# A transformer decoder layer with a routed feed-forward: a new order for the last batches' steps on four engines

## The reference, cut to what matters

```
x = layernorm(x + linear_attention(x))            # 16 heads of 16; inner layer norm; out @ Wo
x = layernorm(x + softmax_cross_attention(x, ctx)) # 16 heads of 16
# feed-forward: 8 experts of 256 -> 512 -> 256, each token goes to its best 2
g      = gelu(xt @ wg1 + bg1);  probs = softmax(g @ wg2)
gates  = top-2 of probs
y      = sum_e gates[:, e] * (gelu(xt @ w_in[e]) @ w_out[e])
x = layernorm(x + y)
```

## Time and profile before

| what | value |
|---|---|
| median of 3 runs | 430.15 us (430.11 to 433.9) |
| the profiled execution's own time | 431.93 us |
| its span | 430.1 us (1.83 us of its time lie around the span) |
| mean granted TensorE clock | 0.923 of full speed |
| busy: PE, DVE, ACT, POOL | 81%, 72%, 52%, 51% of the span |

### The profile page before, as it was taken

How to read it: one execution, slowest core, us unless ns; L and a number is a source line. 1 busy time by engine, 2 the same in 40 slices (tenths; PEclk the granted TensorE clock), 3 DMA queues, 4 the chain that set the end, 5 groups by cost and what they waited for, 6 DMA issues and landing times. The chain is left out here.

```text
span 430.1 us, 12345 instructions
## 1 busy us (share of the span) xinstructions
PE 347.9 (81%) x4025; PEld 281.0 (65%) x4025; DVE 308.3 (72%) x912; ACT 222.1 (52%) x518; POOL 220.7 (51%) x287
## 2 busy tenths in 40 slices
PE   2977999999999999999887185759999999999200
PEld 1655777777777877777664053547899999988100
DVE  3767899888988889888777077468677666755193
ACT  3435676667666676766763045353544444444034
POOL 8335456676666766667258554643133333422273
PEclk9999999999999999999898588569999999999855
DMA  7520022220122211221012222325525322321393
GB/s 219 179 76 27 2 75 75 75 77 21 56 75 77 75 39 38 76 75 50 2 53 100 87 77 79 109 76 151 156 81 155 84 69 61 98 75 39 124 378 122
DMA packets 21387, 38.35 MB, mean 89 GB/s; under 512 B 3696, under 2 KB 11120, under 8 KB 21328
## 3 DMA queue, kind: packets, MB, share of 16 engines
q1 hardware_dynamic: 16768, 26.06, 19.8%
q0 software_dynamic: 3408, 9.41, 6.1%
q10 hardware_dynamic: 1152, 2.10, 1.3%
HBM read 24.71 MB, written 12.84 MB: 87 GB/s over the span
## 5 line engine op out<-in xcount | busy, mean ns | idle before, releaser
L575 POOL DMA_INDIRECT parts<-QKT,rows_all x39 | 37.8, 969 | 76.1 <-DVE QKT L1207 65.9
L328 PE MATMUL bank<-QS,EW 128*128 128x256 f16 (+1 forms) x384 | 62.6, 265 | 5.6 <-DVE XB L1021 5.6
L491 POOL TENSOR_TENSOR rstd<-veps,neghalf 128x1 f32<-128x1 f32 x48 | 39.6, 824 | 41.6 <-DVE veps L844 41.2
L1382 PE MATMUL bank<-EW,QV 128*128 x312 | 48.7, 273 | 1.8 <-DVE R L1199 0.8
L328 PE MATMUL bank<-XB,EW 128*128 128x256 f16 (+1 forms) x192 | 49.0, 264 | 0.0
L1199 DVE TENSOR_TENSOR R<-scratch,QV 128x512 f16<-128x512 f32 x39 | 26.7, 691 | 29.4 <-ACT scratch L764 17.9
L1126 DVE TENSOR_REDUCE NM<-bank 128x4 bf16<-128x512 f32 x64 | 39.6, 678 | 11.1 <-remote 10.1
L328 PEld LDWEIGHTS bank<-QS,EW 128*128 x384 | 37.7, 102 | 11.6 <-issue 6.1
L764 ACT ACTIVATE scratch<-bank 128x512 f32<-128x512 f32 x39 | 23.4, 600 | 40.5 <-PE bank L328 38.5
L506 POOL DMA_INDIRECT bkt<-REC,dest x32 | 32.9, 1029 | 21.3 <-issue 11.9
L699 ACT ACTIVATE rows_all<-bank 128x512 f32<-128x512 f32 x64 | 33.2, 603 | 18.2 <-remote 10.8
(11 more groups left out here) (240 smaller groups left out, 941.4 us busy)
## 6 DMA issues: line engine op xcount, KB each, us to landing
scratch<-w_in SPq DMA_DIRECT2D x8, 512.0 KB, 3.3
scratch<-w_out SPq DMA_DIRECT2D x8, 512.0 KB, 3.8
rows_all<-bkt SPq DMA_DIRECT2D x15, 262.0 KB
XC<-x SPq DMA_DIRECT2D x16, 128.0 KB, 3.3
XC<-ctx SPq DMA_DIRECT2D x16, 128.0 KB, 3.2
EW<-parts SPq DMA_DIRECT2D x8, 256.0 KB, 6.8
EW<-parts ACTq DMA_DIRECT2D x8, 256.0 KB, 7.4
out<-rows_all SPq DMA_DIRECT2D x8, 256.0 KB, 2.1
```

The source lines that it names most:

```text
L328: last = pe.matmul(dst, a(c), b(c), start=(c == 0 and i == 0), stop=(c == n - 1 and i == 2))
L491: pool.tensor_tensor(rstd[n][p][:], veps[n][p][:], neghalf[:, 0:1], ALU.pow).then_inc(s_rs[n], 1)
L575: pool.indirect_dma_start(parts, bass.IndirectOffsetOnAxis(ap=home[:, t, f:f + 1], axis=0), Y[t % 2][:, f, :], None).then_inc(s_put[t % 2] ...
L1382: last = pe.matmul(bank[4 + t % 2][:, f * D:(f + 1) * D], a[t % 2][:, h, f * P:(f + 1) * P], b[:, h, :], start=(h == 0 and i == 0 and f == 0),
```

## The change

Three lists are reordered; no computation is added or dropped. `up` is split into two calls of two hidden chunks each, so that other steps can stand between.

```diff
 # POOL, tail
-"sc:0 sc:1 pw1:15 sc:2 sc:3 sc:4 sc:5 sc:6 sc:7 sc:8 pw2:12 sc:9 sc:10 sc:11 sc:12 sc:13 sc:14 pw2:13 "
+"pw1:15 sc:0 sc:1 sc:2 sc:3 x1b:15 sc:4 sc:5 pw2:12 sc:6 sc:7 sc:8 sc:9 sc:10 sc:11 pw2:13 sc:12 sc:13 sc:14 sc:15 sc:16 "
...
 # DVE, tail
-"mx0:14 mx1:14 n1:15 mx2:14 mx3:14 R2:12 s2:12 full:0 O2T:13 nr:13 full:1 QM1:15 full:2 mx0:15 mx1:15 mx2:15 "
+"mx0:14 n1:15 mx1:14 mx2:14 mx3:14 R2:12 s2:12 O2T:13 nr:13 QM1:15 full:0 n2:12 mx0:15 mx1:15 mx2:15 "
...
-"choice1:2 low:0 choice2:2 whose:0 gate1:2 dest:2 gate2:2 low:1 whose:1")
+"choice1:2 choice2:2 gate1:2 dest:2 gate2:2 whose:0 low:1 whose:1")
...
 # PE
-            def up(t, e):
+            def up(t, e, hs=range(HC)):
...
-                for h in range(HC):
+                for h in hs:
...
-                last.then_inc(s_up, 1)
+                if HC - 1 in hs:
+                    last.then_inc(s_up, 1)
...
-                     "x2T:13 cntpre:1 gh:13 ao2:15 x2T:14 lg:1 x2T:15 gh:15 cnt:1 lg:2 turn:0 cntpre:2 up:0 turn:1 cnt:2")
+                     "x2T:13 cntpre:1 gh:13 ao2:15 x2T:14 lg:1 x2T:15 gh:15 turn:0 cnt:1 cntpre:2 lg:2 upa:0 cnt:2 turn:1 upb:0")
```

More of the change, by code:

```diff
@@ L564, in _ @@
                      "pw0:14 qn:15 n1:14 x1b:14 n2:11 nr:12 pw0:15 "
[2 rows of a table removed]
+                     "pw1:15 sc:0 sc:1 sc:2 sc:3 x1b:15 sc:4 sc:5 pw2:12 sc:6 sc:7 sc:8 sc:9 sc:10 sc:11 pw2:13 sc:12 sc:13 sc:14 sc:15 sc:16 "
+                     "pw2:14 sc:17 sc:18 sc:19 pw2:15 "
                      "sc:20 sc:21 sc:22 sc:23 sc:24 sc:25 sc:26 sc:27 sc:28 sc:29 sc:30 sc:31")
@@ L1184, in _ @@
                      "QM1:14 R1:15 s1:15 "
-                     "mx0:14 mx1:14 n1:15 mx2:14 mx3:14 R2:12 s2:12 full:0 O2T:13 nr:13 full:1 QM1:15 full:2 mx0:15 mx1:15 mx2:15 "
-                     "R2:13 n2:12 mx3:15 s2:13 ewl:15 O2T:14 nr:14 ewl:16 R2:14 n2:13 s2:14 ewl:17 O2T:15 nr:15 n2:14 R2:15 s2:15 "
-                     "choice1:1 n2:15 choice2:1 gate1:1 dest:1 gate2:1 "
-                     "choice1:2 low:0 choice2:2 whose:0 gate1:2 dest:2 gate2:2 low:1 whose:1")
+                     "mx0:14 n1:15 mx1:14 mx2:14 mx3:14 R2:12 s2:12 O2T:13 nr:13 QM1:15 full:0 n2:12 mx0:15 mx1:15 mx2:15 "
+                     "mx3:15 R2:13 s2:13 full:1 O2T:14 nr:14 full:2 n2:13 ewl:15 ewl:16 R2:14 s2:14 ewl:17 O2T:15 nr:15 R2:15 s2:15 n2:14 "
+                     "choice1:1 n2:15 choice2:1 gate1:1 dest:1 gate2:1 low:0 "
+                     "choice1:2 choice2:2 gate1:2 dest:2 gate2:2 whose:0 low:1 whose:1")
             def hidden_low(t):
@@ L1637, in emit @@
                     tile_turn(b)
-                if step == "up":
+                if step == "upa":
                     pe.wait_ge(s_tables, 1)
@@ L1641, in emit @@
                     held[b] = expert_of(b)
-                    up(b, held[b])
+                    up(b, held[b], range(0, HC // 2))
+                if step == "upb":
+                    up(b, held[b], range(HC // 2, HC))
                 if step == "cntpre":
```

## The result

| | kernel before | changed kernel |
|---|---|---|
| median of 14 runs each | 431.11 us | 438.35 us |
| ratio | | 1.0151, 95% interval 1.0118 to 1.0185 |
| profiled execution, own time | 431.93 us | 437.45 us |
| its span, mean granted clock | 430.1 us, 0.923 | 435.7 us, 0.921 |

What follows compares the result with a forecast made beforehand. PE was taken to bound the loop, its start delayed by signals held during scatter runs. Up to `up:0`: -3.6 + 2.3 - 1.2; then -3.1 + 2.2 - 0.5 = -1.4 us, so 428.7 us median, range 421.5 to 433.5.

Steps and rivals of the forecast that it cites:

- The first gap: ACT's and DVE's idle stretch ahead of `ex:14` and `mx:15`: forecast to end at 242.7, 3.6 us earlier.
- until the run has drained: Inferred mechanism: PE's signals are held in a long run of POOL scatters until its end; the gaps ended 1.8 and 1.6 us behind.
- the hold swallows: Some 3 us gained by batch 15 from `pw1:15` ahead of the scatters lies ahead of the hold and was counted as 0.
- POOL, rest of group 0: Behind `pw2:13`, eight scatters instead of five: 3.8 us more work; tile 0 lands about 266, still ahead of `turn:0`.
- 6 to 8 us in: How far into a long run of scatters PE's signals were taken to begin being held, inferred from two gaps.
- DVE, behind the first gap: DVE's weight splits and other moved steps ahead of `R2:14` make `n2:15` 2.3 us later behind the gap, bounds 1 and 3.2.
- PE, turn to product: PE from `n2:15` to `up:0`: `turn:0` ahead of `cnt:1` and `low:0` ahead of `choice1:2` give -1.2 us, bounds -2.5 and 0.
- The second gap: Wait ahead of `high:1` and `dest:2`: `up:1` at 278.3, run of 12 scatters holds `turn:2` to 286.9; sum -1.4 us.
- I let it pass: The signal of `up:0`, 6.9 us into the run of 12 scatters, was assumed not held, so `down:0` follows `up:1`.
- a rival at 0.17 with 433.4: The signal of `up:0` is held too: gelu at 286.9, `down:0` +1.0 at 289.8, low clock +2.3; chance 0.17.
- My own sign for this case: `down:0` starting after 289 in the profile would show that the signal of `up:0` is held too.
- the scatters don't cause the gaps: Rival: the gap ahead of `ex:14` ends at 246.37 by another cause, +2.3 on DVE and -1.2 on PE stay; 431.3, chance 0.08.

Runs made afterwards that it cites:

- all12_behind_b: Changed kernel with POOL waiting for the signal of `up:0` ahead of scatter 20, so the last twelve scatters follow it; held 436.78 us (1.0153), free 426.21 us (1.0229).
- pool_only: Kernel before with POOL's new order alone; free 414.72 us (0.9976) and 414.60 us (0.9966), held, as `pool_only_c`, 431.29 us (0.9967).
- pe_only: Kernel before with PE's new order and the two halves of the first product alone; free set, 417.99 us (1.0047).
- after_ewl15_c: Changed kernel with `ewl:15` back ahead of `full:1` and `O2T:14` in DVE's list; free 415.35 us (0.9979), held 437.39 and 436.80 us (1.0115, 1.0122).
- dve_ewl15: Kernel before with DVE's new order alone, but `ewl:15` back ahead of `full:1` and `O2T:14`; held set, 439.84 us (1.0169).

## Why the prediction was wrong

- **The first gap.** That the scatters hold signals up is borne out by `all12_behind_b`, and the gap moved with the list. That a signal stays held "until the run has drained" is not. The end came at 240.1, forecast 242.7: the last scatter started at 239.36 (forecast 240.0) and ended at 240.32, and `ex:14` did not wait for that end, let alone 1.8 us behind it. The trace of before already had a case that I passed over. ACT's `QM0:15` ended a wait with no releaser named in mid-row, while scatters ran on until 244.55, and PE's own `nat:15` was not through before 243.63, so DVE's wait ahead of `mx:15` was not for a signal alone:

```profile
234.79 0.81 ACT L686 ACTIVATE QM<-bank,bq2m,mask 128x128 f32<-128x128 f32 x2 [3.08 <-remote]
...
243.36 0.27 PE L1537 MATMUL bank<-K,QM 32*128 32x128 bf16 x1 [0.47 <-issue]
```

That POOL's new order gives batch 15 some 3 us ahead of the gap, which "the hold swallows" and I counted as 0, is seen in the free sets: 3.4 us (`ex:14` at 230.97 in `pool_only`, 234.36 in `pe_only`). Held, nothing of it is left: with `lns:13` late, PE starts `q2:15` at 232.71, before at 230.59.
- **The step that failed first: "POOL, rest of group 0".** I moved three scatters behind `pw2:13`, priced them as work (+3.8 us) and a shared port (the scatters beside the two splits took 0.96 and 1.03 us, so the port cost next to nothing), and never asked which signal of PE would fall beside them. `sc:15` did: 4.6 us of waiting, so -6.3 became -1.4. My onset of "6 to 8 us in" came from two gaps and was no rule: `sc:15` was held 2.5 us into its run. So the 3.6 us that I booked as gained are not there at `n2:15`: `pool_only_c` has it at 265.0, before 265.5 and 265.0.
- **"DVE, behind the first gap": +2.3, bounds 1 and 3.2.** From the gap's end to `n2:15` the changed kernel takes 8.7 us more (27.8 against 19.1), 4.9 of them up to `ex:15`, which is the held `sc:15`, and 3.8 behind it. I listed DVE's own instructions and forgot what `ewl:15` issues: SP's load, and behind it ACT's `ewh:17` and `lns:15`. Free, DVE's order costs from `ex:14` to `n2:15` 4.2 us more than POOL's alone (26.1 against 21.9), and 3.6 of it is this word. With the word back, 0.6 is left from `ex:14` on, under my lower bound, so the prices that I did set were too high there. Held, `ex:15` to `n2:15` grew by 3.8 us (15.2 against 11.4). With the word back the stretch is 0.9 us shorter in one pair and 0.6 longer in the other.
- **"PE, turn to product": -1.2 was right** (7.88 to 6.37 us from `n2:15` to `up:0`, -1.5), but only with DVE's half of it.
- **"The second gap": the signal of `up:0`, "I let it pass", was the largest error.** `up:0` ended 5.6 us into the run and was held. I had this as a rival at 0.17 with 433.4. Its place and its mechanism were right. Its size was not, because I took the run as starting at 270.4 "as before": `dest:1` hangs on `n2:15` and PE's counts, so it started at 273.72 and the hold ended at 290.8 and not 286.9. `down:0` was +5.0, not +1.0, and the half clock behind it added 2.2, as I had reckoned (+2.3). My own sign for this case, `down:0` after 289, came with 293.8.
- **The rival "the scatters don't cause the gaps"** is wrong where signals are held, and right that scatters alone are not enough: free sets have the same scatters and no gap. That could not be seen from one profile.

So in the held kind the marks put the loss at the held `up:0` (+4.1 us from `up:0` to `down:0`) and the half clock behind it (+2.2), on top of an `up:0` that is 0.9 to 2.4 us late itself. That is read from traces; no run with DVE's and PE's new orders gets it back in a held set. In the free kind it is the weight split, and `after_ewl15_c` shows it. `ewl:15` back takes away all of +0.75% where nothing is held, and 0.25% and 0.42%, within the noise, of some 1.5% where signals are. POOL's order alone is the only part that was run in both kinds, and it is slower in neither.

## What to carry to other kernels

Before a step moves in one engine's list, write down what it releases on the queues as well: a buffer freed late is a late load, and the engine that waits for the load has unrelated work behind it. Where a wait ends in "remote", compare its end with the time at which the awaited engine ended the work: here that told a late signal from late work. Then ask for each signal what it will fall beside, and look at the short waits of that kind as well as the longest. And when a profile shows such a state, take it as one of at least two, and look whether an order still pays in the other.

## What the runs showed of the hardware

- In held sets PE's signals were 2 to 12 us late while POOL issued indirect scatters 1.26 us apart. The latest ones (`sc:14` in `before`, `up:0` in `after`, `down:0` in `all12_behind_b`) came out 1.8 to 2.1 us behind the last scatter, others in mid-row. A signal of ACT passed in time beside them: in `dve_ewl15` DVE starts at 241.01 on what ACT ended at 240.98, before the row's end at 244.13. In free sets no such delay shows, and the kernel before takes 3.4% less time (416.3 against 431). The cleanest pair is `after_ewl15_b` and `after_ewl15_c`: one kernel on one chip, 436.80 us held and 415.35 free. The kind lasted for a whole set.
- The delay can begin early (`sc:15` in `after`, when two scatters of its row are through) or late (in `before` `x1T:15` still passed 5.5 us in), so no fixed onset shows. In a held stretch PE's own instructions also start late: in the changed kernel PE starts four products between 285.05 and 288.64, and they stand 0.7 and 1.4 us apart.

```profile
285.05 0.37 PE L328 MATMUL bank<-QS,EW 128*128 128x256 f16 x1 [1.15 <-issue]
...
285.78 0.37 PE L328 MATMUL bank<-QS,EW 128*128 128x256 f16 x1 [0.36 <-issue]
...
287.22 0.37 PE L328 MATMUL bank<-XB,EW 128*128 128x256 f16 x1 [1.08 <-issue]
...
288.64 0.37 PE L328 MATMUL bank<-QS,EW 128*128 128x256 f16 x1 [1.04 <-issue]
```

- The Trainium skill ("SBUF — State Buffer", Who interferes with whom) says that PE and ACT never wait on anyone. The section is on SBUF ports. For ACT no run speaks against it. For PE the held sets show signals 10 us and more late, and late starts, beside scatters, whether by a port or by another path: what the path is stays open. It could also be a matter of being profiled. No run here tests that: each of them lists the span that the profiler took.
